# Local attention and gated layers: masks taken off TensorE, and weights and last inputs loaded a stage early

## The reference

```python
h = shift_token(x);  q, k, v = split(h @ wqkv)      # 8 heads of 64
q = l2norm(q) * qs;  k = l2norm(k) * ksc;  q, k = rotary_xpos(q, k)
# windows of 128 tokens; each looks at itself and at the window before it
mask = (i < j) | (i > j + WINDOW) | (j == -1)
attn = softmax(where(mask, -max, 8 * q @ k.T));  x = x + (attn @ v) @ wo
h = layernorm(shift_token(x)) * lg + lb
a, g = split(h @ w1 + b1);  x = x + (a * gelu(g)) @ w2 + b2
```

## Time and profile before

| | |
|---|---|
| Time, median of 3 runs | 3534.86 us (3532.56 to 3538.28) |
| Profiled execution, its own time | 3537.87 us |
| Span of the profiled execution | 3536.2 us |
| Busy: PE, PEld, DVE, ACT, POOL | 89%, 55%, 67%, 49%, 22% |
| Mean granted clock of TensorE | 0.954 of full speed |

### The profile page before, as it was taken

The page is one execution under the profiler, slowest core; times in us unless marked ns, Lnnn a source line. Parts: engine busy times, 40 slices in busy tenths (PEclk is TensorE's granted clock), DMA queues, the critical chain, the costliest instruction groups (busy, mean ns, idle before and its releaser), DMA issues. The chain is left out here.

```text
span 3536.2 us, 76024 instructions
## 1 busy us (share of the span) xinstructions
PE 3162.5 (89%) x31852; PEld 1928.2 (55%) x31852; DVE 2373.5 (67%) x3284; ACT 1722.9 (49%) x3173; POOL 785.7 (22%) x757
## 2 busy tenths in 40 slices
PE   7799999999999999998689999959968999995995
PEld 6433333344443433343467777647856777764784
DVE  7699998987899988772356555535535655553554
ACT  4267777887678888886033333222213333322221
POOL 7400000000110000001043333312224333331221
PEclk9699999999999999997899999979989999997998
DMA  7420001000210000000300000000010000000004
GB/s 242 130 61 17 9 9 45 9 14 13 59 39 9 13 13 5 5 8 23 127 24 14 20 20 14 8 32 0 0 34 24 14 20 20 14 8 32 0 0 143
DMA packets 62014, 113.62 MB, mean 32 GB/s; under 512 B 9608, under 2 KB 25480, under 8 KB 61192
## 3 DMA queue, kind: packets, MB, share of 16 engines
q1 hardware_dynamic: 57608, 102.84, 9.5%
q10 hardware_dynamic: 4096, 6.30, 0.7%
HBM read 74.77 MB, written 33.55 MB: 31 GB/s over the span
## 5 line engine op out<-in xcount | busy, mean ns | idle before, releaser
L649 DVE TENSOR_REDUCE mp<-ps_m 128x2 f32<-128x1024 f32 (+3 forms) x1152 | 1275.7, 1135 | 186.2 <-PE ps_m L700 132.9
L627 ACT ACTIVATE probs<-ps_s 128x512 f32<-128x512 f32 (+3 forms) x2304 | 1162.6, 561 | 372.8 <-PE ps_s L724 342.2
L740 PE MATMUL ps_o<-probs,vall 128*32 128x256 f32 (+3 forms) x9216 | 708.4, 379 | 15.7 <-POOL probs L604 9.1
L724 PE MATMUL ps_s<-qst,kst 64*128 64x512 f32 (+3 forms) x2304 | 593.0, 484 | 4.5 <-ACT probs L627 3.1
L700 PE MATMUL ps_m<-kst,qst 64*128 64x512 f32 (+3 forms) x2304 | 479.1, 399 | 33.4 <-DVE mp L649 15.8
L724 PEld LDWEIGHTS ps_s<-qst,kst 64*128 64x128 f32 x2304 | 240.7, 186 | 457.2 <-ACT probs L627 399.3
L740 PEld LDWEIGHTS ps_o<-probs,vall 128*32 128x32 f32 x9216 | 185.5, 109 | 339.8 <-issue 175.3
L700 PEld LDWEIGHTS ps_m<-kst,qst 64*128 64x128 f32 x2304 | 231.8, 191 | 78.0 <-DVE mp L649 58.7
L989 POOL TENSOR_TENSOR a_rot<-a_t 128x512 f32<-128x512 f32 x128 | 163.0, 1273 | 448.6 <-DVE a_t L1344 448.6
L1514 ACT ACTIVATE m_gl<-m_bank_u,m_b 128x512 f32<-128x512 f32 x96 | 66.3, 691 | 344.4 <-PE m_bank_u L77 344.4
L1035 ACT ACTIVATE a_sq<-a_BP 128x512 f32<-128x512 f32 x128 | 76.6, 599 | 292.8 <-PE a_BP L77 292.8
(11 more groups left out here) (182 smaller groups left out, 5271.3 us busy)
## 6 DMA issues: line engine op xcount, KB each, us to landing
a_tab<-in_rope SPq DMA_DIRECT2D x32, 512.0 KB
q_parts<-pparts SPq DMA_DIRECT2D x32, 256.0 KB, 3.9
k_parts<-pparts SPq DMA_DIRECT2D x32, 256.0 KB, 3.9
qst<-q_parts SPq DMA_DIRECT2D x64, 128.0 KB, 2.6
o_raw<-o_sb SPq DMA_DIRECT2D x32, 256.0 KB, 2.1
X<-in_x SPq DMA_DIRECT2D x8, 512.0 KB, 6.1
kst<-k_parts SPq DMA_DIRECT2D x32, 128.0 KB, 3.7
qst<-q_parts SPq DMA_DIRECT2D x64, 64.0 KB, 2.6
```

What stands on the lines that cost most here:

```text
L627: act.activation(probs[:, s % PR, h, off:C], sslots[n % SR][:, off:C], ACT.Exp, scale=float(D) ** -0.5).then_inc(exp_done, 1)
L649: dve.tensor_reduce(mp[b % 2][:, h:h + 2, cc:cc + 1], slot[:, :, 0:width], AX.X, ALU.max).then_inc(max_read, 1)
L724: pe.matmul(sslots[n % SR][:, off:C], kst[g % 2][rows, hp, i * P:(i + 1) * P], qst[q_slot(b)][rows, hp, off:C], start=True, stop=True).the ...
L740: last = pe.matmul(ps_o[32 * h:32 * h + VW, lo:hi], vall[:, i, (g * GH + h) * DV:(g * GH + h) * DV + VW], probs[:, s % PR, h, lo:hi], star ...
```

## The change

- **Masks.** `mask_unit` is gone from both scorings. In `row_max` the two reductions become eight `tensor_tensor_reduce`, one for each head of the window, which add the fp32 mask from SBUF to 256 scores, write them back to PSUM and give the row's maximum; a `memset` of one element stands ahead of them. In `score_turned` the product with `row1` becomes two products with rows of a table (`rows_own`, `rows_next`), 128 columns each, whose extra rows push every block of 8 masked keys down; the stairs inside a block are cleared afterwards by GpSimd (`trim`: two `affine_select` of 512 elements for each half of a window) in `PT`. `weigh` waits for `trim_done`.
- **Weights.** Two buffers `W` of 3,072 columns live over all layers. `project_out` loads and splits `w_qkv` of layer 0 (ScalarE high, GpSimd low); each local layer loads and splits `w_1` of its MLP behind its last projections (ScalarE in pass 17, VectorE in pass 18); the first MLP loads and splits `w_qkv` of layer 1 in its last slot. `w_o` is split in pass 1, `w_2` in slot 0.
- **Gate.** Y and x are loaded during the second MLP. GpSimd does three of the eight additions.

```diff
             def score_max(w):
                 if w >= 1:
-                    pe.wait_ge(max_done, 2 * w)
+                    pe.wait_ge(max_done, 8 * w)
                 if w >= 3:
                     pe.wait_ge(exp_done, 2 * (w - 2))
-                mask_unit()
...
             def score_turned(kb):
...
-                mask_unit()
                 a = (kb % RW) * P
                 runs = spans(kb, 2 if kb + 1 < NT else 1)
-                for q in range(2):
-                    for at, off, n in runs:
+                for part, rows_by in enumerate((rows_own, rows_next)[0:2 if kb + 1 < NT else 1]):
+                    at = ((kb + part) % RW) * P
+                    for q in range(2):
                         for i in range(4):
                             rows = slice(32 * i, 32 * i + 32)
-                            pe.matmul(SU[:, i, q * N2 + off:q * N2 + off + n], row1[rows, :], negm[rows, q, at:at + n],
-                                      start=False, stop=False, tile_position=(32 * i, 0), skip_group_check=True)
+                            pe.matmul(SU[:, i, q * N2 + part * P:q * N2 + part * P + P], rows_by[rows, :], negm[rows, q, at:at + P],
+                                      start=(part == 0 and q == 0), stop=False, tile_position=(32 * i, 0), skip_group_check=True)
...
             def row_max(w):
...
-                for b in range(2):
-                    dve.tensor_reduce(mx[:, w % 2, 2 * b:2 * b + 2, :],
-                                      SU[:, 2 * b:2 * b + 2, :].rearrange("p i (q c) -> p i q c", q=2)[:, :, :, lo:N2],
-                                      AX.X, ALU.max).then_inc(max_done, 1)
-                dve.wait_ge(max_done, 2 * (w + 1))
+                dve.memset(idle[:, :], 0.0)
+                for i in range(4):
+                    for q in range(2):
+                        dve.tensor_tensor_reduce(SU[:, i, q * N2 + lo:(q + 1) * N2], SU[:, i, q * N2 + lo:(q + 1) * N2], mask[:, lo:N2],
+                                                 1.0, -3.0e38, ALU.add, ALU.max, mx[:, w % 2, i, q:q + 1]).then_inc(max_done, 1)
+                dve.wait_ge(max_done, 8 * (w + 1))
...
+            def trim(kb, b):
+                if win(kb):
+                    pool.wait_ge(exp_done, 2 * kb + b + 1)
+                    part = PT[:, kb % PR, 2 * b:2 * b + 2, :].rearrange("p i (q c) -> p (i q) c", q=2)
+                    own = pool.affine_select(part[:, :, 0:P], part[:, :, 0:P], pattern=[[0, 4], [1, P]], compare_op=ALU.is_ge,
+                                             fill=0.0, base=0, channel_multiplier=-1)
+                    own.then_inc(trim_done, 1)
+                    if kb + 1 < NT:
+                        pool.affine_select(part[:, :, P:N2], part[:, :, P:N2], pattern=[[0, 4], [-1, P]], compare_op=ALU.is_ge,
+                                           fill=0.0, base=0, channel_multiplier=1).then_inc(trim_done, 1)
+
             for k in range(NI + 4):
                 low_part(k - 4, 1)
+                trim(2 * k - 6, 1)
+                trim(2 * k - 5, 0)
                 if live(k):
                     for g in range(4):
+                        if g == 2:
+                            trim(2 * k - 5, 1)
...
+                else:
+                    trim(2 * k - 5, 1)
+                trim(2 * k - 4, 0)
                 low_part(k - 3, 0)
...
                 if q == 0:
                     pe.wait_ge(exp_done, 2 * (2 * p + 2))
+                    pe.wait_ge(trim_done, min(4 * (2 * p + 2), 4 * NT - 2))
...
+                if k == NI + 1:
+                    act.wait_ge(next_in, 16)
+                    act.wait_ge(v_done, NT)
+                    act.activation(W[0][:, :], scr[:, 0:WCOLS], ACT.Copy).then_inc(next_high, 1)
...
+                if k == NI + 2:
+                    dve.wait_ge(next_high, 1)
+                    dve.tensor_tensor(W[1][:, :], scr[:, 0:WCOLS], W[0][:, :].bitcast(F32), ALU.subtract).then_inc(next_low, 1)
...
+            by_pool = (1, 3, 5)        # gate: additions that GpSimd does
```

More of the change, by code:

```diff
@@ L42 @@
 HP = HC * P
+WCOLS = EC * 2 * HP
 def repeat(eng, n, body):
@@ L758, in _, with project_out @@
             weigh(NSTEP - 1, 1)
-def project_out(nc, y_rows, o_raw, w_o, b_o, ident):
+def project_out(nc, y_rows, o_raw, w_o, b_o, ident, w_next, W):
     with ExitStack() as ctx:
@@ L962, in _ @@
                 sp.dma_start(tab[:, :, :], rope[:, k, :, :]).then_inc(tab_in, 16)
+                if k == 0:
+                    sp.dma_start(stage[:, :], w_o).then_inc(wo_in, 16)
+            sp.wait_ge(v_done, NT)
+            sp.wait_ge(ss_done, NI)
+            sp.wait_ge(rot_done, 4 * NI)
+            sp.dma_start(scr[:, 0:WCOLS], w_next).then_inc(next_in, 16)
         @block.gpsimd
@@ L1403, in _, with mlp_layer @@
                 divide(k - 3, 0)
-def mlp_layer(nc, layer, X, w_1, w_2, b_1, ln_cols, b_2, ident, shift, carry):
+def mlp_layer(nc, layer, X, W, w_next, ahead, w_2, b_1, ln_cols, b_2, ident, shift, carry):
     with ExitStack() as ctx:
@@ L1467, in _ @@
         def _(sp):
-            sp.dma_start(stage[:, :], w_1).then_inc(w1_in, 16)
             for dst, src in ((b1_sb, b_1), (ln_sb, ln_cols), (b2_sb, b_2), (id_sb, ident), (sh_sb, shift), (ca_sb, carry)):
                 sp.dma_start(dst[:, :], src).then_inc(const_in, 16)
-            sp.wait_ge(wh_done, 1)
-            sp.wait_ge(wl_done, 1)
-            sp.dma_start(stage[:, 0:HC * E], w_2).then_inc(w2_in, 16)
+            sp.dma_start(stage[:, :], w_2).then_inc(w2_in, 16)
+            if w_next is not None:
+                sp.dma_start(w_f[:, :], w_next).then_inc(next_in, 16)
+            for dst, src in ahead:
+                sp.dma_start(dst, src).then_inc(ahead_in, 16)
+            if ahead:
+                sp.wait_ge(ahead_in, 16 * len(ahead))
         @block.gpsimd
@@ L1682, in _ @@
                 act.activation(part(sg, c), part(X, c), ACT.Silu).then_inc(silu_done, 1)
+        @block.gpsimd
+        def _(pool):
+            for c in by_pool:
+                pool.wait_ge(prod_done, c + 1)
+                pool.tensor_tensor(part(sg, c), part(Y, c), part(x0, c), ALU.add).then_inc(pool_sum, 1)
         @block.vector
```

188 lines of the change are left out of this document (107 added, 81 removed).

## The result

| | before | after |
|---|---|---|
| Time, median of 4 runs | 3533.7 us (3531.4 to 3538.3) | 3439.2 us (3430.8 to 3448.2) |
| Ratio, 95% interval | | 0.9727 (0.9705 to 0.9750) |
| Profiled execution, own time (span) | 3537.9 (3536.2) | 3442.1 (3440.4) |
| Mean granted clock | | 0.954 |

What follows compares the result with a forecast made beforehand. TensorE was taken to run nearly through in the local layers, VectorE and ScalarE close behind. Local passes -25, weights -26.0 and -26.2, gate -11 sum to -88 us, giving 3447 us; range 3408 to 3510.

Steps and rivals of the forecast that it cites:

- taking four masks off TensorE: Local layer pass: masks of 0.96 to 0.97 us each, 3.9 us together; forecast gain 0.97 us a pass.
- the formula: Local layer pass: 9.61 + R + max(12.03, 8.55 + R) + 7.85, forecast 33.69 us against 34.66 before.
- R: Length of one row maximum on VectorE, eight operations: 8p + 0.08, forecast 3.84 us against 2.36 for two reductions.
- p: Cost of one `tensor_tensor_reduce` on VectorE, pass over 256 elements plus delivery: 0.39 to 0.54 us, taken as 0.47.
- the rival of cheap maxima: Local layer maxima: p near 0.39, TensorE binds the pass's second half; -118 us, 3417 us; chance 0.21.
- the stretch from pass 15 on: Local layer's end: last four passes lose seven masks (6.8 us), add three open maxima (3 x 1.48) and `w_1`'s split (3.36).
- the case of the other side: Slower than before: maximum at half rate or held longer, from p = 0.66, 4.3 us per 0.01; chance 0.09.
- the trims at nothing: GpSimd's selects in the local layer, eight a pass, 6.4 us together, costed at nothing; 38 us if uncovered.
- the starts: Earlier weight loads: each local layer begins work 13.0 us sooner, each MLP 13.1 us sooner.
- the split of `w_1` at the end: Local layer, pass 18: in VectorE's queue ahead of `divide(14, 1)`, which the output projection awaits; costs 3.36 us.
- so I charge nothing: `project_out`: 1.5 MB load ahead of the stores, GpSimd's subtraction ending about 2 us before the last store lands; cost 0.
- the gate ends at 25 us: Gate: loads moved beside the second MLP, VectorE keeps 13 operations, about 17.7 us; stage 11 us shorter, near 25 us.

Runs made afterwards that it cites:

- e4: Changed kernel with each masked maximum in two steps, eight additions written back to PSUM, then the two old reductions: 3557.8 us, ratio to before 1.005.
- e3: Changed kernel with one more reduction of 1,024 elements, result unused, ahead of each row maximum: 3489.5 us, ratio to before 0.986.
- e8: Changed kernel without GpSimd's trims and TensorE's wait for them: 3440.4 us, ratio to before 0.973.
- e1: Changed kernel with masks back on TensorE, two old reductions and no trims; loads, splits and gate kept as changed: 3479.5 us, ratio to before 0.983.
- e5: Changed kernel with the weight load in `project_out` issued after the inputs of two chunks instead of all eight: 3438.9 us, ratio to before 0.973.
- e10: Changed kernel with the weight load in `project_out` in six pieces from ScalarE's queue: 3442.6 us, ratio to before 0.974.
- e7: Changed kernel with all eight additions of the gate on VectorE, none on GpSimd: 3435.0 us, ratio to before 0.972.
- e2: Changed kernel with the two old reductions over unmasked scores for the maxima, and a factor 0.25 in the exponential: 3423.1 us, ratio to before 0.967.

## Why the prediction came out as it did

**Right: that taking four masks off TensorE gives far less than their 3.9 us.** The two chains of the formula were there. TensorE waited in the first half of a pass for maxima, division and V, ScalarE had no pause, and the formula, fed with the measured R, gives 32.7 against 32.80. At R = 4.3 and 5.2 it stays within 0.3 us, at 2.35 within 0.6; its two halves miss by 0.3 to 0.4 us in opposite directions.

**Wrong in size: p, the price of one `tensor_tensor_reduce`.** Forecast 0.47 us, measured 0.38, just below the lower end given (0.39), so R = 3.2 instead of 3.84 and a pass 1.8 us shorter instead of 0.97. Both parts of its middle were too high. The pass over the scores costs 0.33 (e4), the row of additions from SBUF in the earlier trace rows, not the 0.39 of the form in the earlier trace rows that has an input in PSUM and a scalar; an input in PSUM by itself costs nothing more. The delivery was put at 0.06 to 0.15 on top, and most of its 0.145 lies beside the next pass. The Trainium skill, "VectorE: DVE Perf Modes", section "Two Vector instructions with no wait between them", has the accumulator's reading as an instruction of its own; the trace agrees (512 of them, 145 ns), but its length isn't its price. This is the rival of cheap maxima, to which 0.21 was given. It forecast 3417; the time was 3439, as its -55 us in the layers behind their starts were -40, and `project_out` took 6.4. So the forecast, with p too high, came nearer than the rival that had p right.

**Left out: the clock at the end of a layer.** By the prediction's own terms at R = 3.2 the stretch from pass 15 on should have been 2.9 us shorter than before (-2.0 for pass 15, -6.8 for seven masks, +2.5 for three maxima, +3.4 for the split); it was 1.8 longer in layer 0 and 1.9 in layer 1, so 9.5 us were missing over both. The rows of that stretch, before and after, show one reason that no term had: the granted clock. Of 106.5 us 10 went by at 1.2 GHz before (0.95), and of 108.3 us 17 after (0.92), behind longer waits: 3.29 us instead of 2.48 for the maxima, 6.34 instead of 2.32 for the low part of the output. How much of the 9.5 us is the clock and how much the waits was not separated.

```profile
2231.90:2338.40 106.50, 90.48 (x1396) 69.37 (x1388) 50.23 (x66) 25.89 (x39) 22.94 (x16) 0.95 0.01 2
```

```profile
2205.10:2313.40 108.30, 82.50 (x1380) 68.02 (x1372) 56.84 (x139) 28.19 (x41) 43.12 (x46) 0.92 0.05 16
```

**Right in kind, low in size: the case of the other side.** The forecast had the kernel slower than before from p = 0.66, that is R = 5.4. Between e3 (R = 4.3, 3489.5) and e4 (5.2, 3557.8) the time rises by 76 us for each us of R and crosses 3534 near R = 4.9, p = 0.60. The mechanism was right; the price of 4.3 us per 0.01 was low (0.08 x 76 = 6.1), as a pass rose by 2.5 us per us of R instead of 2, and the ends of the layers with it. In the passes the rest is the clock behind the longer wait, as the rows of e4 show. The prediction's sums for a dear p don't come out of its own terms either: they give +5 us for both layers at p = 0.54, not +9, and 3503 at p = 0.60, not 3509 (and -53, not -55, at 0.39); the forecast itself isn't touched. The rule that the prediction took from the Trainium skill, "VectorE: DVE Perf Modes", section "The DRAIN you can't avoid", by which the next operation starts only when the pipeline is empty, would have given 0.46 us or more from start to start; the trace shows 0.38 for the new operation and 0.33 for additions. The same section goes on that a next operation which is not held starts earlier, and with that the trace agrees.

**Right: the trims at nothing** (e8), **the starts** (-14.4 a local layer where -13.0 was forecast, -13.0 for MLP 0 where -13.1 was), **the split of `w_1` at the end** (3.36 forecast, +3.2 and +3.7 in e1). Not foreseen was that GpSimd's subtraction of the output is stretched from 1.26 to 3.64 us beside it, and ends 1.1 us after it:

```profile
2284.49 3.35 DVE L1397 TENSOR_TENSOR Wl<-a_scr,Wh 128x3072 fp32r<-128x3072 f32 x1
```

```profile
2285.31 3.64 POOL L992 TENSOR_TENSOR a_oTl<-a_on,a_oTh 128x512 fp32r<-128x512 f32 x1 [3.65 <-ACT a_oTh L1071]
```

**Wrong: `project_out`, "so I charge nothing".** The working looked only at when GpSimd's subtraction would end against the last store, and had it 2 us ahead; it was 0.4 ahead of a store that itself landed 6 us late. The load was not set against the input stream and the stores. 1.5 MB beside them cost 5 to 6 us wherever they were put (e5, e10).

**Wrong: the gate ends at 25 us.** It took 27.8. The working had GpSimd's three additions free and VectorE's at 1.22; they hold each other for 3.25 us. With all on VectorE, e7, the stage is 25.5 us. That this is what was forecast for the shared form is chance: 16 operations took 19.3 us where 13 had been given 17.7, and behind the last were 3.7 us, not 5.

## What to carry to other kernels

When an engine is relieved, write the time of one pass as a sum with a max() over the chains of the other engines, and feed it with the one price that is not known; here it came within 0.3 us in three kernels and 0.6 in a fourth over a doubling of R, and told which reordering pays. Check its terms as well as its sum, and read them from several passes. An operation that is moved to another engine or queue has three prices: its own length, what is queued behind it, and what it does to those with whom it shares a memory path; the last was missed twice here. Price an operation that the trace doesn't have by the plainest row with the same elements, and a second instruction behind it by what it keeps from starting, not by its length.

## What the runs showed of the hardware

- A VectorE operation that also writes an accumulator is two instructions in the trace, 0.46 and 0.145 us; the second overlaps the next operation, and eight follow each other at 0.38 us.
- VectorE with one operand in PSUM and one in SBUF, result in PSUM: 0.33 us from start to start for 256 elements, as from SBUF to SBUF.
- Two-input operations of GpSimd and VectorE, both in SBUF, hold each other: 1.23 to 3.25 us for 1,024 elements on VectorE, and 1.26 to 3.64 for GpSimd's 512 beside a long one of VectorE. A VectorE operation with one input, of 8 elements, went from 0.18 to 0.60 beside GpSimd's subtraction (e2). In each of the three the later one ends last, as if they took turns. Beside VectorE operations that read PSUM, GpSimd's subtraction of 3,072 elements took its 6.7 us and VectorE's stayed at 1.28 for two (e5). GpSimd's selects were not seen to hold anything.
- The granted clock of TensorE fell to 1.2 GHz in a wait of 3.3 us, and how long it stayed there went with up to 4 us at the end of a layer between runs of the same code. Behind waits of 2.46 us the next products were slow in eight of ten passes (e4), behind 1.54 us in none of ten (e3).
- DMA engines that are shown as busy for 26% of the time had no room for 1.5 MB more without delay to the stream that kept them so; that stream had four packets under way at every moment.
